# The matrix fill of a graph kernel: one-hots compared four at a time, weights on ScalarE, stores split three to one

## The reference

```
def _L2_gnn_ref(emb, edge_weight, row, col, num_layers):     # row = src, col = dst
    w = edge_weight[:, None]
    X = emb
    for _ in range(num_layers):                              # 3
        msgs = w * X[col]
        X = jax.ops.segment_sum(msgs, row, num_segments=n)
    return X
```

## Time and profile before

| | us |
|---|---|
| median of 3 runs | 10508.26 |
| lowest and highest | 10503.42, 10534.5 |
| the profiled execution | 10509.52 |
| its span | 10507.6 |
| busy in it: TensorE, VectorE, GpSimd, ScalarE | 7619.7, 7188.9, 5226.6, 1582.9 |

### The profile page before, as it was taken

How to read it: one execution, slowest core, us unless ns; L and a number is a source line. 1 busy time by engine, 2 the same in 40 slices (tenths; PEclk the granted TensorE clock), 3 DMA queues, 4 the chain that set the end, 5 groups by cost and what they waited for, 6 DMA issues and landing times. The chain is left out here.

```text
span 10507.6 us, 173882 instructions
## 1 busy us (share of the span) xinstructions
PE 7619.7 (73%) x34427; PEld 5671.4 (54%) x34428; DVE 7188.9 (68%) x12981; ACT 1582.9 (15%) x4852; POOL 5226.6 (50%) x6235
## 2 busy tenths in 40 slices
PE   0888859899997777656666559766664986666398
PEld 0788859788875444324444346544443664444266
DVE  2233346699965777405888779788877978887698
ACT  0222211233320000001111011211111121111011
POOL 1677730377754888503777500277770007777100
PEclk9999999899998999867999789799987979999698
DMA  5333351122231333573555631255573115555510
GB/s 23 52 60 61 60 53 40 35 46 46 46 32 56 110 110 110 201 289 111 137 137 137 111 72 31 59 137 137 137 125 76 37 33 137 137 137 134 93 37 23
DMA packets 1413037, 947.03 MB, mean 90 GB/s; under 512 B 916254, under 2 KB 1276695, under 8 KB 1412434
## 3 DMA queue, kind: packets, MB, share of 16 engines
q0 software_dynamic: 184960, 458.42, 20.2%
q1 hardware_dynamic: 1131794, 427.96, 17.2%
q10 hardware_dynamic: 96192, 59.54, 1.8%
HBM read 697.23 MB, written 248.11 MB: 90 GB/s over the span
## 5 line engine op out<-in xcount | busy, mean ns | idle before, releaser
L845 PE MATMUL ps<-rows,ohT 128*128 x7040 | 2178.6, 450 | 1346.1 <-DMA gx<-table_g,gi 668.2
L629 POOL DMA_INDIRECT gx<-table_g,gi x2640 | 2503.1, 948 | 802.6 <-issue 726.2
L845 PEld LDWEIGHTS ps<-rows,ohT 128*128 128x128 f32 x7040 | 1448.0, 248 | 1915.0 <-DMA gx<-table_g,gi 976.9
L1134 PE MATMUL ps<-work,oh 128*128 128x273 f32 (+1 forms) x7040 | 1778.9, 408 | 345.0 <-DVE oh L648 336.9
L1134 PEld LDWEIGHTS ps<-work,oh 128*128 128x128 f32 x7040 | 1340.7, 228 | 782.2 <-issue 434.9
L614 POOL COPY gi<-src_i 128x16 int32 (+1 forms) x280 | 57.6, 206 | 2466.4 <-POOLq L508 2404.2
L734 DVE TENSOR_TENSOR work<-gx,ps 128x768 f32<-128x768 f32 x660 | 629.8, 954 | 732.5 <-PE ps L847 731.7
L1099 DVE TENSOR_TENSOR work<-rows,xl 128x1024 f32<-128x1024 f32 (+1 forms) x880 | 871.6, 991 | 319.1 <-DMA xl<-xs_g 146.6
L795 ACT CAST ohT<-ps 128x512 f32<-128x512 bf16 x888 | 520.2, 586 | 3639.9 <-PE ps L828 3622.2
L629 POOL DMA_INDIRECT gx<-table_r,gi x880 | 833.0, 947 | 269.9 <-issue 207.4
L629 POOL DMA_INDIRECT gx<-table_t,gi x880 | 832.7, 946 | 264.7 <-issue 209.9
(11 more groups left out here) (307 smaller groups left out, 9331.6 us busy)
## 6 DMA issues: line engine op xcount, KB each, us to landing
big<-dense_d SPq DMA_DIRECT2D x96, 784.0 KB
dense_d<-big SPq DMA_DIRECT2D x588, 98.0 KB
dense_d<-big ACTq DMA_DIRECT2D x588, 98.0 KB
gx<-table_g,gi POOLq DMA_INDIRECT x2640
xs_g<-gx SPq DMA_DIRECT2D x660, 64.0 KB
xl<-xs_g SPq DMA_DIRECT2D x660, 64.0 KB, 1.8
rows<-dense_d SPq DMA_DIRECT2D x48, 784.0 KB
type_d<-work SPq DMA_DIRECT2D x220, 96.0 KB
```

Of the source, the lines that this page charges most:

```text
L629: pool.indirect_dma_start(m.gx[:, u, k, 0:w], None, table, bass.IndirectOffsetOnAxis(m.gi[:, odd, u * K + k:u * K + k + 1].bitcast(U32), 0 ...
L845: ins = nc.tensor.matmul(to, turned, rows, start=True, stop=not adds)
L1134: ins = nc.tensor.matmul(sums(u), m.oh[:, u, k, :], rhs(u % 2)[:, k, :], start=(k == 0), stop=(k == K - 1))
```

## The change

- VectorE compares the `v_key` of all four visits of a turn in one instruction of 512 columns (L1591 of the changed kernel, `place`). The row of node numbers for it is copied once into PSUM; the result, unweighted, goes to `m.ohT`, in two halves that alternate by turn. It also makes the fourth of the four high one-hots (`last_high`, L1598).
- ScalarE multiplies each 128 columns by its weight (`scale`, L1657) into `spots`, which now has 8 slots.
- GpSimd makes three high one-hots a turn in place of four.
- The sums (`add`, L1606) follow each other in the program, four in a row.
- SyncE stores slots 0, 1 and 2 and loads the four homes of a turn with one load and four checks (L1703 to L1710); ScalarE's queue stores slot 3 (L1661 to L1663).
- TensorE's idle product has 256 columns in place of 512.
- On VectorE, ScalarE and TensorE the loop holds two turns; on GpSimd and SyncE one.

```diff
--- before.py
+++ after.py
@@ -1567,12 +1567,15 @@
 
 def dense_fill(nc, m):
 
-    spots = m.one_hots[:, 0:RING * P].rearrange("p (n q) -> p n q", n=RING)
-    at = RING * P
+    places = m.ohT
+    spots = m.one_hots[:, 0:2 * RING * P].rearrange("p (n q) -> p n q", n=2 * RING)
+    at = 2 * RING * P
     his = m.one_hots[:, at:at + RING * HIS].rearrange("p (n h) -> p n h", n=RING)
     sums = m.big[:, 0:RING * HIS].rearrange("p (n h) -> p n h", n=RING)
-    filler = m.iota_b[:, :].unsqueeze(1).to_broadcast([P, K, P])
-    turns = VISITS // RING
+    filler = m.iota_b[:, :].unsqueeze(1).to_broadcast([P, K, P])[:, 0:2, :]
+    node_no = m.ps[:, 5, 0:P]
+    stored_rows = m.dense_d.rearrange("(w p) h -> w p h", p=P)
+    turns, last = VISITS // RING, RING - 1
 
     def before(u):
         return (u + RING - 1) % RING
@@ -1583,6 +1586,18 @@
 
         @block.vector
         def _(dve):
+            def place(i, half):
+                need(dve, s("spots"), (i - 1) * RING)
+                nc.vector.tensor_tensor(
+                    places[:, half, :].rearrange("p (n q) -> p n q", n=RING),
+                    node_no.unsqueeze(1).to_broadcast([P, RING, P]),
+                    m.v_key[:, bass.ds(i * RING, RING)].unsqueeze(2).to_broadcast([P, RING, P]),
+                    ALU.is_equal).then_inc(s("places"), 1)
+
+            def last_high(i):
+                nc.vector.tensor_scalar(his[:, last, :], m.hi_no[:, :], m.v_hi[:, bass.ds(i * RING + last, 1)], None,
+                                        ALU.is_equal).then_inc(s("last_high"), 1)
+
             def add(i, u):
                 v = i * RING + u
                 dve.wait_ge(s("made"), v + 1)
@@ -1592,18 +1607,25 @@
                                                scalar=m.v_keep[:, bass.ds(v, 1)], in1=m.ps[:, u, 0:HIS],
                                                op0=ALU.mult, op1=ALU.add).then_inc(s("summed"), 1)
 
-            def body(i, u):
-                v = i * RING + u
-                need(dve, s("made"), v - RING + 1)
-                nc.vector.tensor_scalar(spots[:, u, :], m.iota_row[:, :], m.v_key[:, bass.ds(v, 1)],
-                                        m.v_w[:, bass.ds(v, 1)], ALU.is_equal, ALU.mult).then_inc(s("hot"), 1)
-                if u:
-                    add(i, u - 1)
-                elif not isinstance(i, int) or i:
-                    add(i - 1, RING - 1)
-            nc.vector.memset(sums[:, RING - 1, :], 0.0)
-            groups(dve, body, turns)
-            add(turns - 1, RING - 1)
+            def turn(i, odd, more=True):
+                if more:
+                    place(i + 1, 1 - odd)
+                for u in range(RING):
+                    add(i, u)
+                if more:
+                    last_high(i + 1)
+            nc.vector.memset(sums[:, last, :], 0.0)
+            nc.vector.tensor_copy(node_no, m.iota_row[:, :]).then_inc(s("numbers_set"), 1)
+            dve.wait_ge(s("numbers_set"), 1)
+            place(0, 0)
+            last_high(0)
+            for i in range(2):
+                turn(i, i % 2)
+            with dve.Fori(2, turns - 2, 2) as i:
+                turn(i, 0)
+                turn(i + 1, 1)
+            turn(turns - 2, 0)
+            turn(turns - 1, 1, False)
 
         @block.gpsimd
         def _(pool):
@@ -1611,8 +1633,10 @@
 
             def body(i, u):
                 v = i * RING + u
+                if u == last:
+                    return
                 if not u:
-                    need(pool, s("high"), v)
+                    need(pool, s("high"), i * last)
                     nc.gpsimd.tensor_copy(numbers, m.v_hi[:, bass.ds(v, RING)]).then_inc(s("numbers"), 1)
                     pool.wait_ge(s("numbers"), i + 1)
                 need(pool, s("made"), v - RING + 1)
@@ -1621,38 +1645,74 @@
                                         ).then_inc(s("high"), 1)
             groups(pool, body, turns)
 
+        @block.scalar
+        def _(act):
+            def scale(i, odd):
+                act.wait_ge(s("places"), i + 1)
+                act.sem_inc(s("turn_act"), 1)
+                for u in range(RING):
+                    v = i * RING + u
+                    need(act, s("made"), v - 2 * RING + 1)
+                    act.sem_inc(s("spot_act"), 1)
+                    nc.scalar.activation(spots[:, odd * RING + u, :], places[:, odd, u * P:(u + 1) * P], ACT.Copy,
+                                         scale=m.v_w[:, bass.ds(v, 1)]).then_inc(s("spots"), 1)
+
+            def store(i):
+                home = act.value_load(m.v_home[0:1, bass.ds(i * RING + last, 1)], min_val=0, max_val=NWIN + RING - 1)
+                act.wait_ge(s("summed"), i * RING + RING)
+                act.dma_start(stored_rows[bass.ds(home, 1)].rearrange("a p h -> (a p) h"), sums[:, last, :]
+                              ).then_inc(s(f"stored{last}"), 16)
+            scale(0, 0)
+            for i in range(2):
+                scale(i + 1, (i + 1) % 2)
+                store(i)
+            with act.Fori(2, turns - 2, 2) as i:
+                scale(i + 1, 1)
+                store(i)
+                scale(i + 2, 0)
+                store(i + 1)
+            scale(turns - 1, 1)
+            store(turns - 2)
+            store(turns - 1)
+            act.wait_ge(s(f"stored{last}"), 16 * turns)
+
         @block.tensor
         def _(pe):
-            def body(i, u):
+            def body(i, u, odd):
                 v = i * RING + u
-                pe.wait_ge(s("hot"), v + 1)
-                pe.wait_ge(s("high"), v + 1)
+                pe.wait_ge(s("spots"), v + 1)
+                if u == last:
+                    pe.wait_ge(s("last_high"), i + 1)
+                else:
+                    pe.wait_ge(s("high"), i * last + u + 1)
                 need(pe, s("summed"), v - RING + 1)
-                nc.tensor.matmul(m.ps[:, u, 0:HIS], spots[:, u, :], his[:, u, :], start=True, stop=True
+                nc.tensor.matmul(m.ps[:, u, 0:HIS], spots[:, odd * RING + u, :], his[:, u, :], start=True, stop=True
                                  ).then_inc(s("made"), 1)
-                nc.tensor.matmul(m.ps[:, RING + u, :], m.ident_b[:, :], filler, start=True, stop=True)
-            groups(pe, body, turns)
-
-        def store(eng, slots):
-            def body(i, u):
-                if u not in slots:
-                    return
-                v = i * RING + u
-                home = eng.value_load(m.v_home[0:1, bass.ds(v, 1)], min_val=0, max_val=NWIN + RING - 1)
-                eng.wait_ge(s("summed"), v + 1)
-                eng.dma_start(m.dense_d.rearrange("(w p) h -> w p h", p=P)[bass.ds(home, 1)].rearrange("a p h -> (a p) h"),
-                              sums[:, u, :]).then_inc(s(f"stored{u}"), 16)
-            groups(eng, body, turns)
-            for u in slots:
-                eng.wait_ge(s(f"stored{u}"), 16 * turns)
+                nc.tensor.matmul(m.ps[:, 4 + 2 * (u % 2), 0:2 * P], m.ident_b[:, :], filler, start=True, stop=True)
+            for v in range(2 * RING):
+                body(v // RING, v % RING, v // RING)
+            with pe.Fori(2, turns, 2) as i:
+                for odd in range(2):
+                    for u in range(RING):
+                        body(i + odd, u, odd)
 
         @block.sync
         def _(sp):
-            store(sp, (0, 2))
-
-        @block.scalar
-        def _(act):
-            store(act, (1, 3))
+            def body(i, u):
+                if not u:
+                    homes[:] = nc.values_load_multi_w_load_instructions(
+                        m.v_home[0:1, bass.ds(i * RING, RING)], engines=(mybir.EngineType.SP,),
+                        min_val=0, max_val=NWIN + RING - 1)[1]
+                if u == last:
+                    return
+                sp.wait_ge(s("summed"), i * RING + u + 1)
+                sp.sem_inc(s("turn_sp"), 1)
+                sp.dma_start(stored_rows[bass.ds(homes[u], 1)].rearrange("a p h -> (a p) h"), sums[:, u, :]
+                             ).then_inc(s(f"stored{u}"), 16)
+            homes = []
+            groups(sp, body, turns)
+            for u in range(last):
+                sp.wait_ge(s(f"stored{u}"), 16 * turns)
 
 
 def dense_layers(nc, m):
```

## The result

The changed kernel takes 10,606.6 us (median of 4 runs, 10,602.3 to 10,612.0) against 10,510.5 before (4 runs, 10,503.4 to 10,534.5; the 10,508.3 that the prediction starts from is the median of the first three). The ratio is 1.0088 with a 95% interval of 1.0070 to 1.0105: slower, and by +96 us where the prediction had +44.

A forecast was written before the change was run, and what follows sets the result against it. GpSimd's four comparisons were taken to set the fill's 3.66 us turn; SyncE's 3.81 would replace it, +0.15 x 294 = +44 us, from a profiled 10,509.5 to 10,553.5, or 10,552 as median; range 10,490 to 10,605.

The forecast's parts named there:

- SyncE's 2.85: In the fill before the change, SyncE's own instructions take 2.85 us a turn, beside 0.81 us of waiting for sums.
- The signs named beforehand: In the fill: turns near 3.8, SyncE hardly waiting, late sums on VectorE, GpSimd idle some 0.9 a turn, about 105 GB/s.
- SyncE's sum of 3.77: SyncE's turn in the fill: old 2.85, plus store 0.60, increments 0.21 and two checks 0.50, less a load 0.39.
- a load of four values for which there is no row: SyncE's single load of a turn's four homes, an uncertainty named for the 3.81 us turn; loads were priced 0.27 to 0.41.
- The 0.04 added to reach 3.81: SyncE's turn in the fill, taken as 3.81 us between estimates of 3.77 and 3.93, with ends 3.70 and 3.95.
- The bounds of 0.27 to 0.41: The price in us of a load on SyncE, used in its sum for the turn.
- The upper estimate, from the edge loop's loads and issues: SyncE's turn from the edge loop's 5.54, less three loads 1.18 and one issue 0.64, plus increments 0.21: 3.93 us.
- The price of a store: One more store on SyncE costs 0.60 us with registers, number waited on and gaps; three increments cost 0.21.
- Put at 3.39: VectorE's turn in the fill: 3.39 us, with sums 0.65 apart and a 196-column comparison of 0.4 to 0.5.
- The rival in which VectorE decides: In the fill SyncE's sum is 0.4 or more too high, VectorE sets 3.39 a turn: 10,429 us, chance 0.20.
- The lock-out, rival 3: VectorE's 196-column comparison waits out a whole GpSimd operation in SBUF: turn 3.94, +82 us, 10,590; chance 0.08.
- the fourth rival: TensorE's clock falls with the shorter idle product, a price only above 3.5 a turn, so nothing; no separate chance.

The follow-up runs named there:

- The control without checks: The kernel before with the range checks of its stores left out on SyncE and ScalarE, all else as it was: ratio 1.0000.
- the stores' part alone: The kernel before with only the stores split three to one, SyncE loading and checking four homes at once: 10,620.6 us, ratio 1.0087.
- the run without increments: The changed kernel with three checks, four homes loaded, SyncE's loop of two turns, and SyncE's three semaphore increments removed: 10,393.8 us, ratio 0.9883.
- the run without checks: The changed kernel with the four range checks on SyncE's homes left out and nothing else: 10,396.1 us, ratio 0.9868.
- The run split two to two: The changed kernel with slots 0 and 2 stored by SyncE, 1 and 3 by ScalarE's queue: 10,591.9 us, ratio 1.0061.
- The run with 512 columns: The changed kernel with TensorE's idle product back at 512 columns: 10,621.8 us, ratio 1.0087.

## Why the prediction was right, and where it was off

**What bounded the kernel before: right.** The prediction read GpSimd's four comparisons as the turn and SyncE's 2.85 beside it. The control without checks (ratio 1.0000) shows that SyncE did not set it; that GpSimd did rests on its trace, in which it waits for itself alone.

**The sign and the mechanism: right.** The path went from GpSimd to SyncE's queue. The signs named beforehand are there: SyncE with 3.4 us of wait in place of 239.3, sums that start late, GpSimd idle 1.2 a turn of 3.945 (361.9 us in all for TensorE; 0.9 had been forecast), 103 GB/s in place of 109 (105 had been forecast). That the stores' part alone gives 1.0087, and that the turn follows SyncE's sum down through 4.04, 3.945, 3.718, 3.483 and 3.215, settles it.

**The size: too small by half, and the step is the load.** The turn grew by 0.286 in place of 0.15, so the fill by 84 and not 44 us. The median of 10,606.6 is just past the upper end of the range; by the ratio, 10,508.3 x 1.0088 = 10,601, it is inside. SyncE's sum of 3.77, taken as 3.81 in the forecast, came out at 3.945. The term that failed is "a load of four values for which there is no row". The sum kept for it one load of one value behind the loop's branch, 0.41; its mean is 0.50. That is 0.09 of the 0.175 that the sum lacks. The rest is small terms: 0.03 in the old turn's 2.85 (SyncE's own instructions and gaps in that trace make 2.88, if each store's registers have the gap of 0.03 ahead of them that they have in the run without increments, where hardly anything is waited for); 0.02 in the two checks; 0.02 in register operations and their gaps; 0.01 in the increments. The 0.04 added to reach 3.81 covered half of these.

The four values are not all of the load's 0.09. Where SyncE had time to spare, in the run without checks, the same load took 0.428 to 0.451, 0.03 above one value behind the branch. In the changed kernel 90 of the 210 loads in the stretch of 830 us took 0.50 or more. Why they did was not found.

The bounds of 0.27 to 0.41 that I had for the load came from loads of another form; they should not have been its ends. The upper estimate, from the edge loop's loads and issues, gave 3.93: the better of the two, although I gave it less weight. It holds a load of one value as well, and the turn passed it though it was called an upper end, so that it came so near is in part luck.

**The price of a store: right.** The prediction took 0.60 for the issue with its registers and gaps, and 0.07 for each increment. The run split two to two has 0.70 together. The issue alone holds SyncE's queue for 0.340 to 0.344 in the 868 rows above.

**VectorE: 0.2 too high.** Put at 3.39, it set 3.18 where SyncE was out of the way. Its dependent sums start 0.62 apart, not 0.65, and its 196-column comparison takes 0.32, not 0.4 to 0.5. The rival in which VectorE decides had it too dear, but its condition (SyncE below 3.55) did not come true.

**The lock-out, rival 3: wrong.** The 196-column comparison on VectorE, beside a GpSimd that was busy for 62% of the fill:

```profile
L1598 DVE TENSOR_SCALAR oh<-gx,big x289: 314/317/512, 3304.5 to 4442.3; 128x196 f32<-128x196 f32 x145
```

Its median is 3 ns off its minimum. Four in five of these comparisons stood beside one of GpSimd for more than half of their time (median 0.331, up to 0.512); the others took 0.314 to 0.319. So they are somewhat longer beside GpSimd, but the longest is 0.2 above the shortest, while one comparison of GpSimd takes 0.77: no whole comparison was ever waited out. The Trainium skill, "SBUF — State Buffer", section "Who interferes with whom", speaks of a full block until the first is done, for the engine that asks second for the ports that both share. No run here tells whether this comparison asks for them.

**The clock: it fell and cost nothing, as the fourth rival had it.** The run with 512 columns, where it mostly did not fall (0.98), is no faster.

**ScalarE: hidden, as forecast, but thinner.** A scaling takes 0.386 alone and four take 1.28, not 1.1:

```profile
L1657 ACT ACTIVATE oh<-ohT,big x1176: 384/386/403, 3288.4 to 4444.5; 128x128 f32<-128x128 f32 x196
```

In the changed kernel that is covered. In the split of two to two it was not: I had 2.4 plus 1.2 for the second store, 3.6, and the turn took 3.85, of which the dearer scalings are 0.18.

## What to carry to other kernels

A queue that only issues transfers is an engine like the others: add up everything that it executes, loads, range checks, increments, loop ends and gaps, before it is given another transfer. Here an engine relieved of a quarter of its work gave nothing, since a queue with 0.8 us of slack a turn was handed 1.1 us of serial instructions in the same change; taking 0.7 us of them out again, with the check of every home that is stored to kept, turned +0.88% into -1.17%. And the term of a sum for which the trace has no row needs an upper bound from outside the rows that look like it.

## What the runs showed of the hardware

- **A load of three values into registers takes longer than one of four.** 0.800 to 0.971 us for three, 0.430 to 0.592 for four, in the same place; without a branch ahead the medians are 0.86 and 0.30. Why was not tried, nor were two values.
- **A load behind a branch is slower.** Without increments four values take 0.295 to 0.302 inside the loop's body, and 0.43 to 0.46 as the first load after the branch. In the kernel before one value took 0.262 to 0.271 without a branch ahead and 0.400 to 0.419 behind it.
- **A range check is 0.26 us on SyncE**: 0.152 of register operations, 0.018 for the check, and two gaps of some 0.045. Four of them in a turn cost the changed kernel some 225 us.
- **An increment that carries a wait** costs 0.073 with its gaps; with the wait on the register operation instead, nothing.
- **The end of a loop** costs SyncE 0.24: from the turn's last issue to the next load it is 0.40 with it and 0.16 without. The load behind it is slower by some 0.14 more.
